# Two three-layer programs become one, and relative attention's opening is issued among the channel mix's last batches

## The reference

```python
    x = _layernorm(x + _L0_attn_ref(x, ...), axis=-1)              # retention and a gated MLP ("ret")
    x = _layernorm(x + _L0_xattn_ref(x, ctx_1024, ctx_1024, ...))  # cross attention ("xat")
    x = _layernorm(x + _L0_ffn_ref(x, W_r, W_k, W_v, mu_r, mu_k))  # channel mix ("mix")
    x = _layernorm(x + _L1_attn_ref(x, W_qkv, ..., rel_emb_k, rel_emb_v))  # relative attention ("rel")
    x = _layernorm(x + _L1_xattn_ref(x, ctx_1024, ctx_1024, ...))  # mLSTM cell ("mls")
    x = _layernorm(x + _L1_ffn_ref(x, w_q, ..., keys, down_embed, up_embed))  # peer experts ("per")
```

```python
        # channel mix
        x_prev = jnp.concatenate([jnp.zeros((B, 1, C), x.dtype), x[:, :-1, :]], axis=1)
        xr = mu_r * x + (1.0 - mu_r) * x_prev
        xk = mu_k * x + (1.0 - mu_k) * x_prev
        r = jax.nn.sigmoid(jnp.einsum('btc,dc->btd', xr, W_r))
        k_act = jnp.square(jax.nn.relu(jnp.einsum('btc,dc->btd', xk, W_k)))
        out = r * jnp.einsum('btc,dc->btd', k_act, W_v)
        # relative attention, 16 heads of 16
        dist = jnp.clip(idx[None, :] - idx[:, None], -R, R) + R        # R = 64
        score = jnp.einsum('bhqd,bhkd->bhqk', q, k) + jnp.einsum('bhqd,qkd->bhqk', q, rel_emb_k[dist])
        attn = jax.nn.softmax(score, axis=-1)
        ctx = jnp.einsum('bhqk,bhkd->bhqd', attn, v) + jnp.einsum('bhqk,qkd->bhqd', attn, rel_emb_v[dist])
```

## Time and profile before

| | |
|---|---|
| median of 3 runs | 1827.22 us (1819.28 to 1830.35) |
| span of the profiled execution | 1828.8 us |
| PE busy | 1634.0 us (89%), PEld 1279.0 us (70%) |
| DVE busy | 1176.1 us (64%) |
| ACT busy | 684.1 us (37%) |
| POOL busy | 311.6 us (17%) |
| mean granted TensorE clock | 0.935 of full |

### The profile page before, as it was taken

How to read it: one execution, slowest core, us unless ns; L and a number is a source line. 1 busy time by engine, 2 the same in 40 slices (tenths; PEclk the granted TensorE clock), 3 DMA queues, 4 the chain that set the end, 5 groups by cost and what they waited for, 6 DMA issues and landing times.

```text
span 1828.8 us, 38633 instructions
## 1 busy us (share of the span) xinstructions
PE 1634.0 (89%) x14760; PEld 1279.0 (70%) x14760; DVE 1176.1 (64%) x3829; ACT 684.1 (37%) x1426; POOL 311.6 (17%) x329
## 2 busy tenths in 40 slices
PE   6799996899997678888988889898899999999998
PEld 5677775666655556777776657776788888788876
DVE  3655654455554725666656546548888889889894
ACT  3333332245656245666555443223222223222210
POOL 1443435200000110000112105601010001000100
PEclk8899998999999868999998886799999999999999
DMA  3100000001010278889999960230000000000000
GB/s 125 47 18 18 18 12 18 14 19 29 25 54 30 87 256 310 313 293 327 321 319 325 331 223 13 105 131 2 2 8 7 13 2 13 13 2 13 2 7 13
DMA packets 98502, 177.36 MB, mean 97 GB/s; under 512 B 16144, under 2 KB 82832, under 8 KB 93584
## 3 DMA queue, kind: packets, MB, share of 16 engines
q1 hardware_dynamic: 98320, 174.89, 27.7%
HBM read 92.94 MB, written 81.79 MB: 96 GB/s over the span
## 4 chain that ended last, share of the span: by engine, by line
PE 41%; issue 9%; DVE 6%; DMA 4%; ACT 2%; POOL 1%; DVEq 1%; POOLq 1%; SPq 0%; ACTq 0%
PE bank L104 13%; PE bank L2962 10%; PE bank L2922 3%; PE bank L2949 3%; DMA rel_qr_rows<-later_shared 2%; PE bank L1735 2%; PE bank L1701 1%; DVE later_shared L1587 1%; PE bank L112 1%; PE bank L1722 1%; ACT rel_probs L1503 1%; PE bank L2869 1%; DMA later_shared<-rel_qr_rows 1%; PE bank L2894 1%; PE bank L2296 1%
## 5 line engine op out<-in xcount | busy, mean ns | idle before, releaser
L104 PE MATMUL bank<-per_xT,per_down 128*128 128x256 f32 x1024 | 250.7, 390 | 2.3 <-ACT per_xT L2641 1.6
L2962 PE MATMUL bank<-per_up,per_act_w 128*128 128x256 f32 x1024 | 242.7, 383 | 0.0
L2962 PEld LDWEIGHTS bank<-per_up,per_act_w 128*128 128x128 f32 x1024 | 195.5, 192 | 27.0
L2648 ACT ACTIVATE per_act_w<-bank 128x512 f32<-128x512 f32 x128 | 76.2, 597 | 364.3 <-PE bank L104 329.8
L104 PEld LDWEIGHTS bank<-per_xT,per_down 128*128 128x128 f32 x1024 | 190.4, 192 | 29.9 <-issue 2.7
L1503 ACT ACTIVATE rel_probs<-later_shared,rel_low 128x256 f32<-128x256 f32 x256 | 117.0, 517 | 28.8 <-DVE rel_low L1587 28.7
L1587 DVE CUSTOM_DVE_ANT_0 later_shared<-bank,later_shared 128x256 f32<-128x256 f32 x256 | 95.0, 420 | 38.2 <-PE bank L1701 18.6
L920 DVE TENSOR_REDUCE xat_mx<-bank 128x2 f32<-128x512 f32 x128 | 79.5, 685 | 32.7 <-PE bank L968 32.6
L104 PE MATMUL bank<-ret_x2T,ret_w_in 128*128 128x256 f32 x384 | 93.1, 399 | 7.5 <-issue 7.5
L2628 POOL TENSOR_TENSOR per_sim<-per_sim,per_best_i 128x512 f32<-128x512 f32 x32 | 41.9, 1329 | 332.9 <-DVE per_sim L2766 332.9
L1722 PE MATMUL bank<-rel_band_k,later_shared 32*128 32x191 f32 x512 | 67.3, 391 | 30.5 <-DVE rel_low L1587 23.3
(11 more groups left out here) (365 smaller groups left out, 3202.1 us busy)
## 6 DMA issues: line engine op xcount, KB each, us to landing
rel_qr_rows<-later_shared SPq DMA_DIRECT2D x32, 1024.0 KB, 7.5
rel_p_rows<-rel_probs SPq DMA_DIRECT2D x32, 1024.0 KB, 5.7
later_shared<-rel_qr_rows SPq DMA_DIRECT2D x64, 384.0 KB, 4.7
rel_by_dist<-rel_p_rows SPq DMA_DIRECT2D x64, 384.0 KB, 4.7
per_down<-in_per_down SPq DMA_DIRECT2D x1, 4096.0 KB, 12.7
per_up<-in_per_up SPq DMA_DIRECT2D x1, 4096.0 KB, 13.3
ret_xin<-in_x SPq DMA_DIRECT2D x8, 256.0 KB, 2.9
xat_cT<-in_contextT SPq DMA_DIRECT2D x8, 256.0 KB, 3.0
```

Of the source, the lines that this page charges most:

```text
L104: last = pe.matmul(dst, wt[:, c], src[:, c, :], start=c == 0, stop=c == DC - 1)
L2648: nc.scalar.activation(act_w[m % 2][:, 2 * k:2 * k + 2, :], tiles(bank[3 + k % 2]), ACT.Gelu_apprx_tanh).then_inc(gelu_ready, 1)
L2962: last = pe.matmul(tiles(bank[7])[:, t, :], act_w[n % 2][:, k, t * P:t * P + P], up[:, k, :], start=k == 0, stop=k == COLS - 1)
```

## The change

All six layers become one program with one block, one identity tile and one cleanup. Mix's tiles lie at the other end of SBUF (`side="right"`), so that rel's may lie beside them, and rel's are declared in another order. The semaphores of ret, xat and mix are released and taken again by the later layers: at a given step each of four engines drains and counts up `all_passed`, Pool waits for four and clears the numbers, and every engine waits for `all_cleared` before it first uses one again. This happens for ret's numbers at step 26 of xat, and for xat's and mix's at rel's step 16.

```diff
+    EARLY_TURNS, EARLY_KEYS = 5, 3
+    r_bank, v_bank = bank[6], bank[7]
     def turn_bank(b):
-        return bank[2 + b % 2]
+        return bank[2 + b % 2] if b < EARLY_TURNS else bank[4]
     def k_bank(b):
-        return bank[b % 2]
-    def r_bank(b):
-        return bank[4 if late(b) else 6]
-    def v_bank(b):
-        return bank[5 if late(b) else 7]
+        return bank[b % 2] if b < EARLY_KEYS else bank[5]
...
-                if b >= 2:
+                if b == EARLY_KEYS:
+                    before["sums_taken"](pe)
+                elif b > EARLY_KEYS:
+                    pe.wait_ge(k_act_ready, b)
+                elif b >= 2:
                     pe.wait_ge(k_act_ready, b - 1)
...
+                if b >= 1:
+                    pe.wait_ge(r_ready, b)
+                by_token(pe, tiles(r_bank), mixed[:, b % 2, 0], wr).then_inc(r_mm, 1)
...
+                elif b > EARLY_TURNS:
+                    pe.wait_ge(xT_ready, b)
...
+                if b >= 1:
+                    pe.wait_ge(gated_ready, b)
+                by_token(pe, tiles(v_bank), k_act[:, b % 2], wv).then_inc(v_mm, 1)
```

```diff
+    def take_x(sp, b):
+        before["give_x"](sp, b, xin[:, b % XS], x_loaded[b % XS])
+    def sync(sp):
         load_all(sp, loaded, loads)
         sp.dma_start(wv[:], w["wv"]).then_inc(wv_loaded, 16)
         load_all(sp, late, late_loads)
-        for b in range(1, XS):
-            sp.dma_start(xin[:, b], batch_of(x_in, b)).then_inc(x_loaded[b], 16)
+        yield
+        two_before["work_taken"](sp)
+        take_x(sp, 0)
+        yield
         for s in STEPS:
+            if 1 <= s + 6 < XS:
+                take_x(sp, s + 6)
             if (U := turn_of(s)) is not None:
+                if U == 0:
+                    before["over"](sp)
+                    before["kept"](sp)
...
     def gpsimd(pool):
+        pool.memset(qr[:, :, :, BAND:BAND + P], 0.0)
+        pool.memset(qr[:, :, :, 2 * BAND + P:ROW], 0.0)
+        yield
         for s in STEPS:
+            if x_turn_of(s) == 0:
+                pool.memset(v[:, :, :, :, HD:VW], 1.0)
+                pool.memset(bias[:, :, 0, :, NEAR:SEQ], 0.0)
+            if project_of(s) == 0:
+                pool.memset(bias[:, :, 1, :, 0:REACH], 0.0)
+                pool.memset(probs[:, :, :, SEQ:WIDE - SEQ], 0.0)
+                pool.drain().then_inc(band_ready, 1)
...
     def tensor(pe):
+        yield
+        before["early_banks_taken"](pe)
+        yield
         for s in STEPS:
             if (U := turn_of(s)) is not None:
+                if U == 0:
+                    before["late_banks_taken"](pe)
...
             if (U := values_of(s)) is not None:
+                if U == 0:
+                    before["over"](pe)
```

In `first_layers.chained`, LAST_2 is 41, at which mix's step 3 is issued. The two parts ahead of rel's steps come with mix's steps 0 and 3, and then one step of rel behind each of mix's steps 4 to 8, which are rel's steps -5 to -1:

```diff
+    CLEAR_1, LOADS_4 = GROUPS * nb - 6, LAST_2 - 3
...
+            if s == CLEAR_1:
+                pass_group(0)
+            if s == LOADS_4:
+                wait_cleared(0)
+                next(later_steps)
+            if s == LAST_2:
+                next(later_steps)
-        for steps in (steps_2, steps_3):
-            for _ in steps:
-                pass
+        for _ in steps_2:
+            pass
+        for _ in steps_3:
+            next(later_steps)
```

```diff
+            def passes(n, name, engine):
+                if name == "gpsimd":
+                    engine.wait_ge(passed, 4 * (n + 1))
+                    for numbers in groups[n]:
+                        engine.sem_clear(numbers)
+                    engine.sem_inc(cleared, 1)
+                else:
+                    engine.drain().then_inc(passed, 1)
```

299 lines of the change are left out of this document (158 added, 141 removed).

## The result

Of 14 executions of each kernel on one chip the changed one took 1808.27 us in the median (1798.55 to 1823.04), the one before 1825.41 (1819.28 to 1836.47). The ratio of their times is 0.9908, 95% interval 0.9887 to 0.993: faster by 0.9%, clear of noise and within the 1% that the prediction gave 0.55. The forecast was 1809.2 us. Of the ten executions of its repeat, further down, one took 5298.14 us at a mean clock of 0.298 and is left out of the median there.

A forecast was written before the change was run, and what follows sets the result against it. Mix was taken as bound by TensorE and VectorE in a loop, with rel's pipe fill open behind it. Opening 18.5 us less 0.5 for semaphores gave 18.0; from the 1827.2 median that forecast 1809.2 us, range 1801 to 1818.

The forecast's parts named there:

- Opening: From mix's value product 4 to rel's first bias sum: it comes at 643.1 instead of 661.61, 18.5 us gained.
- Loads moved up: Nine weight DMAs go to SP ahead of mix's fifth x load: 0 us, at most about 1.
- Waits inside the mix: TensorE waits 0.8, 1.8 and 1.3 us in mix's batches 5 to 7, beside rel's first steps.
- Banks: Mix's keys and turns get one bank each from batch 3 or 5 on: cost 0.
- Memsets on Pool: 4.0 us of memsets in three steps slow nobody: cost 0, at most 4.0 us if VectorE stood still.
- Semaphores: Two drains on each of four engines, in xat's step 26 and rel's step 16: 0.25 us each, 0.5 lost.
- Rival A: Gain as summed, TensorE at half clock once, waiting at 640 to 644 us: 15 to 20 us gained; chance 0.66.
- C: Clock falls inside the mix, batches 5 to 7: 4 to 9 us less gained, 1813 to 1818; chance 0.12.
- B: Full clock at the start of rel's loop: 2 us more gained, 1805 to 1807; chance 0.12.
- all later distances the same: Behind the opening, rel's batch period stays 47.4 us and no later distance changes.

The follow-up runs named there:

- the kernel whose wait was 3.50: Changed kernel with rel's steps -5 to 0 one batch earlier, beside mix's steps 3 to 8; ratio to before 0.9914.
- the filler: Changed kernel plus nine unused matmuls behind scores 0, in TensorE's 4.0 us wait; ratio to before 0.9901.
- the kernel with both earlier steps: Changed kernel with rel's steps from mix's batch 3 on, two behind batch 4, none behind 7 and 8; ratios to before 0.99 and 0.9891.
- the kernels with earlier steps: Changed kernel with rel's steps one mix batch earlier, ahead of the mix step they followed, or both; ratios to before 0.9914, 0.9899, 0.99 (again 0.9891).

## Why the prediction was right

The sum was made step by step, and the trace has each step. Times are of the two clocks, which stand 0.24 us apart at VP4:

| step | predicted | measured |
|---|---|---|
| value product 5 behind VP4 | 8.6 | 8.36 |
| wait ahead of the queries; their start | 0.8; 616.85 | 0.58; 617.01 |
| wait ahead of table 0; its start | 1.8; 629.1 | 1.72; 629.35 |
| value product 7 behind VP4 | 29.0 | 28.79 |
| first bias sum behind VP4; its time | 37; 643.1 | 37.02; 643.09 |
| scores 1 behind VP4 | 44 to 45 | 44.25 |
| batch of rel's loop | 47.4 | 47.52 |

*Opening, 18.5 us:* measured 18.5 from trace to trace (18.8 from VP4). The bias was hidden, as put: its loads left at 636.9 (636.5 forecast), and VectorE's own queue opened the sum.

*What it consists of* is where the text stayed coarse. It spoke of one fill that the change removes and never said what early loads would bring without the interleaving. By the kernels with the steps behind the mix, about 15 us of it are the loads and 3.2 to 3.6 the interleaving. A forecast for a kernel with the loads alone would have been wrong had it been read from this text.

*Loads moved up, 0 to 1 us:* 0. Pool waited 6.17 us for the weights and was done at 581.0, before the first rstd at 583.69; the distance from mix's value product of batch 0 to VP4 is 27.38 us (578.69, 606.07), in before 27.35.

```profile
575.85 0.22 POOL L1500 TENSOR_SCALAR rel_minus_own<-rel_cols 128x2 f32<-128x2 f32 x1 [6.17 <-DMA rel_reach_k<-in_rel_reach_k]
```

*Waits inside the mix:* three were forecast (0.8, 1.8, 1.3 us) and came as 0.58, 1.72 and 0.93; 0.39 ahead of value product 5 and 0.67 ahead of scores 0 were not in the text.

*Banks, 0:* 0, by the kernel with the banks alone.

*Memsets on Pool, cost 0:* the price was right, the reason wrong, and so the price was luck. I took it that nobody would be held, for want of a row that showed it. VectorE was held beside memsets: 0.90 instead of 0.73 us at 607.44, and 3.58 us in the kernel with the opening behind the mix, where Pool's four memsets stand back to back from 630.89 to 634.09 and the normalisation starts at 630.98 and runs past them. It was also held beside Pool's addition, which the text did not price in the mix at all: 1.68 us at 615.88. What made both free was slack: VectorE waited 1.93 us for the constants behind the first and 4.49 us ahead of k_act at 624.85 behind the second. The rule that I quoted there, from the Trainium skill, "SBUF — State Buffer", section "Who interferes with whom" (a scalar operation of VectorE in a two-port mode is blocked for the whole length of a GpSimd instruction), agrees with these rows, if the normalisations, which are scalar operations, run in such a mode, which no row shows; I had set it aside. Its other half agrees too: the mixes, with two inputs in SBUF, kept 1.66 us beside memsets and took 2.68 beside the addition, which reads SBUF.

*Semaphores, 0.5 us:* nothing can be seen of it, and 23 more drains on each engine did not lengthen rel's loop by what can be read. As far as is known the right term was 0, the lower bound; the clears and the waits for them were not tried by themselves.

*Clock.* Rival A's fall at 640 to 644 is in the window of that time, with 0.71; by 660 it is 0.50. C did not happen although TensorE waited 0.58, 1.72 and 0.93 us inside the mix. It happened in the kernel whose wait was 3.50, but also in the one with the memsets on VectorE, behind the same 1.72 us. So that C stayed away here was partly luck; with the memsets on VectorE it cost 0.5 us at the first bias sum, not 4 to 9. B's condition was not met, and its price of 2 us stays untested: the filler brought 2.0 us, but by a later fall and not by a clock that stayed up.

*The time.* 18.0 us were forecast from the opening less the drains, and the medians differ by 17.1, with an interval from 12.8 to 20.6 (0.0070 to 0.0113 of 1825.4). The profiled pair differs by 22.1, 9.2 of them in mls and -5.3 in rel's loop, which the prediction had as "all later distances the same". They are the same in instructions, not in the clock and in the waits that go with it. The forecast of 1809.2 stood on the median of three runs before, 1827.2; on the 1825.4 of fourteen the same sum gives 1807.4, and 1808.27 was measured. That the total came within a microsecond is luck, as the interval is 8 us wide; that the first bias sum came within 0.3 us of its forecast is not.

## What to carry to other kernels

At a seam between two programs or layers, first ask which transfers stand in the queue behind the last store of the one ahead, and move those: here that was four fifths of what the opening gained (15.2 of 18.8 us), and it needs no interleaving. Issuing the next layer's first steps among the last ones of a dense loop pays only what it hides, less the waits that it puts into that loop (at most 3.6 us net here). What a step waits for is decided by what stands ahead of it in the other engines' queues: table 0 waited 1.72 and 3.50 us one batch behind its projections, and 0.88 us behind the same batch as they, with no relu and sigmoid of mix in between. And where whole executions differ by 25 us through the clock, distances between two instructions of the same trace tell a microsecond's edit where a median of a dozen does not, provided that a second trace of the same kernel has the same distance (0.01 us apart at the first bias sum of the changed kernel, 1.6 us in the kernel with both earlier steps).

## What had not been expected of the hardware

Pool's memsets, which only write, hold VectorE's two 256-wide normalisations (0.73 us for the pair alone, 0.90 and 3.58 beside them), and Pool's addition, which reads SBUF, does too (1.68). VectorE's four 256-wide mixes, with two inputs in SBUF, are held by the addition, from 1.66 to 2.68 us (615.40 in the kernel with its memsets on VectorE), and not by memsets. A copy out of a bank kept its 0.68 us beside the addition (635.07 and 635.24, in the kernel with the opening behind the mix).

The wait just ahead does not tell whether TensorE's clock falls. Behind 1.72 us of it the mix's next keys ran at the full clock in the changed kernel (1.99 us) and at the half clock in the one with its memsets on VectorE (3.44 us). Behind waits of 0.94 and 1.09 us, and behind one of 3.50, they took 3.02 and 3.57 us in the kernels with earlier steps. In a part of the program that no edit touches, the same work took 56 to 70 us from trace to trace.
